# Linear attention over 16 images: keys between queries and outputs on TensorE, the queries' bias in the exponential's shift, the variance by two small matmuls, the query exponentials ahead of the copy

## The reference

```python
def _gn(v, G=32, eps=1e-05): ...          # mean 0, variance 1 in each group of 2 channels
xn = group_norm(x, gn1_w, gn1_b, 32)
qkv = jnp.einsum('oc,bchw->bohw', qkv_w, xn) + qkv_b[None, :, None, None]
q, k, v = jnp.split(qkv, 3, axis=1)       # 8 heads of 16 channels each
q = q.reshape(B, HEADS, DIM_HEAD, n) * scale
q_norm = jax.nn.softmax(q, axis=-1)       # over the 256 pixels
k_norm = jax.nn.softmax(k, axis=-2)       # over the 16 channels of a head
context = jnp.einsum('bhdn,bhen->bhde', k_norm, v)
out = jnp.einsum('bhde,bhdn->bhen', context, q_norm)
out = jnp.einsum('oc,bchw->bohw', out_w, out) + out_b[None, :, None, None]
out = group_norm(out, gn2_w, gn2_b, 1)    # one group: all channels and pixels of an image
return out + res
...
x = x + block(_gn(x), ...)
```

## Time and profile before

| | us |
|---|---|
| median of three runs | 52.71 (52.54 to 52.72) |
| the profiled execution | 52.49 |
| its span, first to last instruction | 50.7 |
| TensorE busy | 42.6 (84%) |
| VectorE busy | 40.6 (80%) |
| ScalarE busy | 33.5 (66%) |
| GpSimd busy | 28.6 (57%) |
| the chain that ended last: TensorE's share | 63% |
| VectorE's share | 25% |

### The profile page before, as it was taken

How to read it: one execution, slowest core, us unless ns; L and a number is a source line. 1 busy time by engine, 2 the same in 40 slices (tenths; PEclk the granted TensorE clock), 3 DMA queues, 4 the chain that set the end, 5 groups by cost and what they waited for, 6 DMA issues and landing times.

```text
span 50.7 us, 1591 instructions
## 1 busy us (share of the span) xinstructions
PE 42.6 (84%) x511; PEld 31.3 (62%) x511; DVE 40.6 (80%) x132; ACT 33.5 (66%) x111; POOL 28.6 (57%) x66
## 2 busy tenths in 40 slices
PE   2999849899989599999999999999999985995000
PEld 2769448656677448866876884886698464834000
DVE  2056999999999995989999999999999698643830
ACT  0183799998586198777958949876494576468300
POOL 5000670088986988899875864884682790222500
PEclk9999999999999999999999999999999999999985
DMA  0598960000000000000110020020020000031122
GB/s 0 138 192 268 347 249 3 0 0 0 0 0 19 0 0 0 0 0 19 65 38 0 11 99 0 13 104 0 0 92 11 0 13 6 0 104 46 57 104 104
DMA packets 2688, 2.66 MB, mean 53 GB/s; under 512 B 244, under 2 KB 2680, under 8 KB 2680
## 3 DMA queue, kind: packets, MB, share of 16 engines
q1 hardware_dynamic: 2528, 2.49, 15.7%
q10 hardware_dynamic: 152, 0.07, 0.6%
HBM read 1.52 MB, written 1.05 MB: 51 GB/s over the span
## 4 chain that ended last, share of the span: by engine, by line
PE 63%; DVE 25%; issue 6%; ACT 1%; POOL 0%; DVEq 0%; ACTq 0%; POOLq 0%
PE o_ps L568 7%; PE o_ps L605 7%; PE q_ps L473 7%; PE o_ps L582 5%; PE v_ps L507 5%; PE q_ps L546 5%; PE k_ps L507 4%; PE q_ps L543 4%; PE v_ps L497 4%; PE k_ps L497 3%; PE o_ps L620 3%; PE o_ps L593 3%; DVE vs L795 3%; DVE res L856 3%; DVE kmx L752 3%
## 5 line engine op out<-in xcount | busy, mean ns | idle before, releaser
L292 POOL TENSOR_TENSOR orstd<-ve,minus_half 128x1 f32<-128x1 f32 x8 | 4.4, 553 | 6.7 <-DVE ve L838 6.7
L273 POOL TENSOR_TENSOR tree<-ek 128x256 f32<-128x256 f32 x7 | 5.1, 725 | 5.4 <-ACT ek L392 5.4
L402 ACT ACTIVATE eq<-q_ps,nqmax 128x256 f32<-128x256 f32 x16 | 7.4, 473 | 0.2 <-DVE nqmax L770 0.2
L415 ACT ACTIVATE fold<-o_ps,rq 128x65 f32<-128x65 f32 x14 | 3.6, 312 | 5.8 <-PE o_ps L582 5.8
L752 DVE TENSOR_REDUCE kmx<-k_ps 128x32 f32<-128x512 f32 x8 | 5.5, 682 | 0.7 <-PE k_ps L507 0.5
L795 DVE TENSOR_TENSOR vs<-v_ps,rks 128x512 f32<-128x512 f32 x8 | 5.5, 691 | 0.3
L507 PE MATMUL k_ps<-w_all,xn 64*128 64x128 f32 x64 | 5.0, 274 | 0.9 <-DVE xn L726 0.9
L473 PE MATMUL q_ps<-ones 128*128 128x512 f32 x12 | 4.7, 550 | 1.0 <-POOL ones L220 1.0
L761 DVE TENSOR_TENSOR ek<-k_ps,kmx 128x512 f32<-128x512 f32 x8 | 5.5, 681 | 0.1
L770 DVE TENSOR_REDUCE nqmax<-q_ps 128x2 f32<-128x512 f32 x8 | 5.4, 678 | 0.0
L426 ACT ACTIVATE osq<-o_ps,nb 128x256 f32<-128x256 f32 x7 | 3.3, 473 | 2.9 <-PE o_ps L605 2.0
(11 more groups left out here) (97 smaller groups left out, 102.0 us busy)
## 6 DMA issues: line engine op xcount, KB each, us to landing
out_dram<-res SPq DMA_DIRECT2D x8, 128.0 KB, 1.7
x_sb<-x_dram SPq DMA_DIRECT2D x1, 512.0 KB, 5.0
x_sb<-x_dram SPq DMA_DIRECT2D x2, 128.0 KB, 2.3
x_sb<-x_dram SPq DMA_DIRECT2D x1, 256.0 KB, 3.9
w_all<-weights_dram SPq DMA_DIRECT2D x1, 224.0 KB, 3.7
mats<-matrices_dram SPq DMA_DIRECT2D x1, 160.0 KB, 4.9
par_avg<-params_dram ACTq DMA_DIRECT2D x1, 67.0 KB, 2.5
brow<-b_qkv_dram ACTq DMA_DIRECT2D x1, 6.0 KB
```

Of the source, the lines that this page charges most:

```text
L273: nc.gpsimd.tensor_tensor(tree[:], e[:, :, 0:8], e[:, :, 8:16], ALU.add).then_inc(tree_step, 1)
L402: last = nc.scalar.activation(eq[:, p % 3, image, :], q_ps[:, image, 0, :], ACT.Exp, bias=nqmax[:, r, image:image + 1], accum_out=qs[:, p ...
```

## The change

Five edits:

1. The queries' bias is no longer added on TensorE: the two matmuls against `scales` go, and that constant with them. The exponential is over pixels, where a constant per channel cancels, so its shift needs only the maximum of the biased queries less the bias. The kernel now makes q_bias once (GpSimd, from a new column of the parameters) and, per pair, `query_shift(p)` on VectorE, (nqmax - q_bias) + q_bias, into qshift, which `query_exp` takes as its bias.
2. query_shift(0) and (1) are called inside `group_variance(2)` and `(3)`, the others behind `minus_mean(i - 2)` in the loop and behind `scale_values` for the last pair.
3. The variance is two matmuls, one per image, with ssq as the stationary side, spread over 64 columns, and one column of the averaging matrix as data. Before, the 128 x 128 matrix was stationary and ssq the data.
4. In TensorE's loop `keys(i + 1)` stands ahead of `means(i - 2)` and `outputs(i - 2)`.
5. In ScalarE's loop `query_exp(i)` stands ahead of `centred(i - 2)`.

```diff
@@ TensorE
                 wait(pe, qexp_ready, p)
-                pe.wait_ge(b_ready, 1)
                 pe.wait_ge(w_ready, 1)
-                pe.wait_ge(scales_ready, 1)
-                for image in range(2):
-                    nc.tensor.matmul(q_ps[:, image, 0, :], bsplit[rows(image), Q], scales[rows(image), 0:PIX],
-                                     start=True, stop=False, skip_group_check=True)
                 for image in range(2):
                     nc.tensor.matmul(q_ps[:, image, 0, :], w_f[rows(image), Q], xn[rows(image), p % 3, :],
-                                     start=False, stop=True, skip_group_check=True).then_inc(q_done[image], 1)
+                                     start=True, stop=True, skip_group_check=True).then_inc(q_done[image], 1)
...
-                nc.tensor.matmul(var_of(p), mats[:, AVG_IMAGE], of(ssq, r),
-                                 start=True, stop=True, skip_group_check=True).then_inc(var_done, 1)
+                for image in range(2):
+                    ins = nc.tensor.matmul(var_of(p)[rows(image), :],
+                                           ssq[rows(image), r:r + 1].broadcast_to([CHANNELS, CHANNELS]),
+                                           mats[rows(image), 2 * P - 1 if image else P:2 * P if image else P + 1],
+                                           start=True, stop=True, skip_group_check=True)
+                ins.then_inc(var_done, 1)
...
                 queries(i)
+                keys(i + 1)
                 means(i - 2)
                 outputs(i - 2)
-                keys(i + 1)
                 context(i - 1)
@@ ScalarE
-                act.wait_ge(qmax_ready, p + 1)
+                act.wait_ge(qshift_ready, p + 1)
...
-                                                bias=nqmax[:, r, image:image + 1],
+                                                bias=qshift[:, r, image:image + 1],
...
                 squares(i - 2)
+                query_exp(i)
                 centred(i - 2)
-                query_exp(i)
@@ VectorE
+            def query_shift(p):
+
+                if not there(p):
+                    return
+                r = p % 2
+                dve.wait_ge(qmax_ready, p + 1)
+                wait(dve, q_bias_ready, 1)
+                wait(dve, qexp_ready, p - 1)
+                nc.vector.tensor_scalar(qshift[:, r, :], nqmax[:, r, :], q_bias[:], q_bias[:], ALU.subtract,
+                                        ALU.add).then_inc(qshift_ready, 1)
@@ GpSimd
-            nc.gpsimd.memset(scales[:].bitcast(F32), QSCALE).then_inc(scales_ready, 1)
...
+            pool.wait_ge(par_in, DMA)
+            nc.gpsimd.tensor_scalar(q_bias[:], par[:, Q_B:Q_B + 1], QSCALE, None,
+                                    ALU.mult).then_inc(q_bias_ready, 1)
```

More of the change, by code:

```diff
@@ L27 @@
 DMA = 16
-GN1_W, GN1_B, OUT_B, GN2_W, GN2_B, LOW_ROW, PARAMS = range(7)
+GN1_W, GN1_B, OUT_B, GN2_W, GN2_B, LOW_ROW, Q_B, PARAMS = range(8)
 TILE = 64
@@ L71, in attention_kernel @@
         ones = sb("ones", [P, 128], F32R)
-        scales = sb("scales", [P, PIX], F32R)
         wjunk = sb("wjunk", [P, CHANNELS])
@@ L102, in attention_kernel @@
         nqmax = sb("nqmax", [HIDDEN, 2, 2])
+        qshift = sb("qshift", [HIDDEN, 2, 2])
+        q_bias = sb("q_bias", [HIDDEN, 1])
         eq = sb("eq", [HIDDEN, 3, 2, PIX])
@@ L132, in attention_kernel @@
         par_in, mats_in, w_in, b_in = (sem(n) for n in ("par_in", "mats_in", "w_in", "b_in"))
-        half_ready, b_zero, ones_ready, scales_ready = sem("half_ready"), sem("b_zero"), sem("ones_ready"), sem("scales_ready")
+        half_ready, b_zero, ones_ready = sem("half_ready"), sem("b_zero"), sem("ones_ready")
         w_ready, bhigh_ready, b_ready = sem("w_ready"), sem("bhigh_ready"), sem("b_ready")
@@ L153, in attention_kernel @@
         ksum_ready, rks_ready, vs_ready = sem("ksum_ready"), sem("rks_ready"), sem("vs_ready")
-        qmax_ready, qexp_ready, rq_ready = sem("qmax_ready"), sem("qexp_ready"), sem("rq_ready")
+        qmax_ready, qshift_ready, q_bias_ready = sem("qmax_ready"), sem("qshift_ready"), sem("q_bias_ready")
+        qexp_ready, rq_ready = sem("qexp_ready"), sem("rq_ready")
         ctx_done, ctxm_ready, fold_done, fold_ready = (
@@ L693, in group_variance @@
                                         ALU.mult).then_inc(mean_x_ready, 1)
+                if g >= 2:
+                    query_shift(g - 2)
                 dve.wait_ge(dev_ready, g + 1)
@@ L768, in query_max @@
                     dve.wait_ge(q_done[image], p + 1)
-                wait(dve, qexp_ready, p - 1)
+                wait(dve, qshift_ready, p - 1)
                 nc.vector.tensor_reduce(nqmax[:, p % 2, :], q_ps[:, :, 0, :], AX.X, ALU.max,
                                         negate=True).then_inc(qmax_ready, 1)
+            def query_shift(p):
[7 more added lines that the diff above has]
+                                        ALU.add).then_inc(qshift_ready, 1)
             def key_norm(p):
@@ L896, in _ @@
                 minus_mean(i - 2)
+                query_shift(i)
                 finish(i - 3)
@@ L911, in _ @@
             scale_values(PAIRS - 1)
+            query_shift(PAIRS - 1)
             output_scale(PAIRS - 4)
@@ L938 @@
     low_row = np.where(c % 64 < 32, 0.0, -1.0).astype(np.float32)
-    params = np.stack([np.concatenate([arr["L0_conv_" + n]] * 2) for n in names] + [low_row], axis=1)
+    params = np.stack([np.concatenate([arr["L0_conv_" + n]] * 2) for n in names] + [low_row, arr["L0_conv_qkv_b"][:HIDDEN]], axis=1)
     group = (c[:, None] // GROUP_CH == c[None, :] // GROUP_CH) / GROUP_CH
```

## The result

The changed kernel took 56.69 us (median of 4 runs, 55.70 to 57.52) beside 52.72 us for the kernel before on the same chip; the ratio is 1.060, with a 95% interval of 1.053 to 1.067. Two of the four runs, 57.30 and 57.52 us at a lower mean clock, are left out of the ratio; the two others, 55.70 and 56.07 us, put the changed kernel near 55.9 us. The profiled execution took 56.07 us with a span of 54.2 us; before it was 52.49 and 50.7. Forecast: 55.7 us (54.4 to 56.6), slower; the median of all four lies 0.09 above that range, the 55.9 within it.

A forecast was written before the change was run, and what follows sets the result against it. TensorE was taken as the bound, 4.27 us a pair. A pair would become 4.78 (2.56 of chain plus 2.22 of need), the end 3.0 later, so 55.5 us profiled and 55.7 us as median; range 54.4 to 56.6.

The forecast's parts named there:

- The pause: TensorE's loop: it stands still 0.85 us in each pair, the variance waiting for ScalarE's copy.
- The need: Loop: from the end of outputs through squares, exponentials and copy to the earliest variance, 2.22 us.
- The cover: TensorE's loop: context and values, the work left between outputs and variance, 1.37 us.
- The pair: Loop: one pair, from variance to variance, takes 4.78 us against 4.27.
- The variance: TensorE: two 64-column matmuls take 0.21 us instead of 0.31; bounds 0.10 and 0.31.
- The start: Ahead of the loop: two shifts on VectorE cost 0.28 us, folds(0) at 17.32 instead of 17.04; bounds 0 and 0.52.
- Behind the loop: After variance(4) at 41.00: vs at 44.50, folds(7) at about 46.9, the end 3.0 us later.
- The bounds: Whole run: pair 4.57 and end 54.5 us at the low side, pair about 4.95 and end 56.6 at the high.
- With 1 and 2 alone: TensorE's pair with only the queries' bias removed and the small variance: 4.27 - 0.32 - 0.10 = 3.85 us.
- A: Rival: TensorE's 0.42 us a pair is really returned, VectorE becomes the bound, 51.5 us; chance 0.07.
- B: Rival: TensorE's rests drop the granted clock to 1.2 GHz in the loop, 57 to 68 us; chance 0.02.
- C: Rival: no measurable change, pause about half (0.43 us), pair 4.3, 52.9 us; chance 0.02.

The follow-up runs named there:

- e9: Changed kernel, but for pairs 0 to 4 the ScalarE copy reads x in SBUF and the variance no longer waits for it: 52.79 us, ratio 1.004.
- e3: Changed kernel with both moves undone (copy ahead of exponentials, keys behind outputs), keeping the shift and the small variance: 52.73 us, ratio 1.003.
- e4: Kernel before with only the query exponentials put ahead of the copy on ScalarE: 54.13 us, ratio 1.027.
- e5: Kernel before with only the keys put ahead of means and outputs on TensorE: 52.91 us, ratio 1.004.
- e7: Kernel before with only the variance done by two small matmuls: 51.57 us, ratio 0.981.
- after2: The changed kernel once more, unedited, beside the others on the same chip: 56.14 us, ratio 1.063.
- v1: e3 with query_shift left out, query_exp taking nqmax of the queries without bias: 51.51 us, ratio 0.978.
- e6: Kernel before with only the queries' bias moved from TensorE into the shift: 53.28 us, ratio 1.012.
- e2: Changed kernel with the keys behind the outputs again on TensorE: four runs of 53.38, 54.48, 55.87 and 56.05 us, not settled.
- e1: Changed kernel with the copy ahead of the query exponentials again on ScalarE: 53.17 us, ratio 1.011.
- e8: Changed kernel with the variance of a pair taken one turn later, behind the keys, and variance_eps and output_scale moved with it: 56.58 us, ratio 1.071.

## Why the prediction was right, point by point

**The pause.** Predicted 0.85 us ahead of each of five variances, released by the copy; it is 1.10 to 1.13, released by the copy, five times. The need was put at 2.22 and is 2.33; 0.09 of the difference is the release, 0.14 where I took 0.05. The cover was put at 1.37 and is 1.23: context ends at 30.24, 0.47 behind the outputs and not 0.61. That e9 without this wait comes to 52.79 us shows that the pause is the cause.

**The pair.** 4.78 predicted, 4.80 measured. From the variance's start to the outputs' end I had 2.56, and it is 2.47 (27.30 to 29.77); so the mechanism was right, but that the sum came within 0.02 is luck: two errors nearly cancel, 0.09 less of TensorE and 0.11 more need.

**The variance.** I took 0.21, from the means' piece of the chain. Folds follow after 0.13 (27.30 to 27.43). The piece of the chain runs from one end to the next; from start to start the means themselves take 0.14 (29.00 to 29.14). The Trainium skill ("TensorEngine Tiling (Array Packing)", Key Properties), whose rule that tiles work in parallel I had set at 0.10, was nearer than my row. Whether the two halves ran at once the runs don't tell, since 0.13 is what the means take too. In the changed kernel's sum the error is worth 0.08 a pair.

**The start.** Folds(0) at 17.32 predicted, 17.79 measured. At 0.47 this is the largest missed size of the sum. The 0.75 over the kernel before has two parts. The second shift moved its successor by 0.34 instead of 0.14; no row says why it costs more than the first. The other 0.42 stand at the end of pow_in, and they are not the first shift's 0.15: pow_in ends with GpSimd's addition, before and after, and the addition came 0.42 later, behind ScalarE's key exponentials (10.01 for 9.57), on an engine whose first squares of the input started at 6.57 for 5.99. e3, with the same instructions up to the loop, had these squares at 6.25, the addition at 10.39, pow_in in 0.40 and folds(0) at 17.49. So the two shifts cost 0.45 there where I had 0.28, inside my bound of 0.52, and some 0.3 came with the later addition, for which the sum had no term. That the change itself delays the input is not shown: the squares start between 5.99 and 6.90 in the four profiles without the shift and its parameter (before, e4, e5, e7), between 6.20 and 6.64 in the others.

**Behind the loop.** Variance(4) at 41.70 for 41.00: 0.47 of it is the start, 0.13 pair 0, 0.10 the four pairs. The new lateness was seen rightly: shift behind vs (45.51), the exponentials until 46.85, variance(5) waiting for them at 46.99, folds(7) at 47.30 for 46.9. From variance(4) to vs it took 3.22 instead of 3.50, so 0.3 of the lateness was made good. The last variance gave nothing back in this profile: 0.38, in a window at 0.53 of the clock; in after2 the same line is 0.28. Ends: 3.6 later for 3.0, 56.07 for 55.5.

**The bounds.** The upper one does not come out of its own terms: 0.10 for the variance and 0.08 make the pair 4.96 before anything is added for the releases, and five such pairs with 0.24 more at the start end near 56.8, not 56.6.

**An argument that failed off the sum.** "With 1 and 2 alone TensorE's pair would be 3.85" is wrong. v1, which has those savings and nothing on VectorE against them, has 4.04, and e6 shows where 0.3 of it stay: in the wait for the fold copy. It did no harm to the forecast, because keys ahead of the means fill this wait (27.43 to 29.00 is 1.57, and the copy needs about 1.0).

**The rivals.** A, faster because the copy doesn't bind, fell. Its point of decision, the copy over within 1.37 of the outputs' end, was the right one: it is over at 2.19. Its next bound was right too: e9 takes the copy's wait away and finds VectorE, 4.22 in A's 3.85 to 4.26, near its upper end. B, the clock: not in the loop's pauses, where the windows say 1.00. But the half clock at the start of the loop in e2's profile is B's mechanism at a place that I had not looked at. C fell with the exponentials' 0.45 each; half the pause would by the sum have been a pair of 4.36 and 53.6 us, not C's 4.3 and 52.9.

## What to carry to other kernels

Before an instruction is moved, write down for the wait behind it how long its releaser needs and how much work covers it; two moves that each fit the slack can overdraw it together, and the loss then comes at once and in every turn. An instruction taken from the engine that is always busy saves only what no other wait takes back: look for the next operand that comes late (here the fold copy, then VectorE) ahead of counting the gain. And ask whether a correction is needed at all: leaving the shift out of e3 gave 1.2 us. Whether another place for it would have been as good was not tried.

## What the runs showed of the hardware

**A small VectorE instruction that meets GpSimd's addition lasts until the addition ends.** The changed kernel, e1 and e3 have the same instructions up to the loop, and in all three pow_in starts at 10.76, while the addition starts when ScalarE's key exponentials are over, which differs from profile to profile. In e3:

```profile
10.76 0.40 DVE L711 TENSOR_SCALAR pow_in<-gvar 128x2 f32<-128x2 f32 x1
```

```profile
10.39 0.75 POOL L274 TENSOR_TENSOR tree<-ek 128x256 f32<-128x256 f32 x1 [3.08 <-ACT ek L396]
```

The addition starts at 10.39 in e3, 10.60 in e1 and 10.70 in the changed kernel; pow_in takes 0.40, 0.60 and 0.69 and ends 0.02 behind the addition each time (11.16, 11.36 and 11.45). In e9 the addition starts at 10.77, pow_in slips in ahead of it in 0.17, and the instruction behind it is the one that takes 0.71. In after2 the addition is early (10.34): there the instruction behind the shift (dev), at 10.38, takes 0.71 where it took 0.15, and without the shift it would have started before the addition. The shift itself takes 0.28 us at 10.20, before the addition starts, 0.57 in e3's loop, and 0.61 in e8, where the rows are:

```profile
34.40 0.61 DVE L787 TENSOR_SCALAR qshift<-nqmax,q_bias 128x2 f32<-128x2 f32 x1
```

```profile
34.27 0.72 POOL L274 TENSOR_TENSOR tree<-ek 128x256 f32<-128x256 f32 x1
```

They end at 35.01 and 34.99. Not every instruction is held: gvar, with one operand in o_ps, takes 0.16 at 10.57 in e3, in the middle of the addition. No run moved the addition by an edit, but the same instruction ends with it wherever it lies. The Trainium skill ("SBUF — State Buffer", "SBUF: two separate sides") has a rule that fits: VectorE and GpSimd share one pair of ports, which GpSimd or a VectorE instruction in a two-port mode or with two inputs in SBUF holds for its whole instruction, whichever starts first, while the other blocks. The rows ahead of the loop agree with it; in e3's loop the shift has the earlier start (32.26 against 32.36) and is held all the same, so who comes first can't always be read from the starts. A small instruction so costs what is left of the large one beside it: 0.29 and 0.33 us more for the shift, some 0.5 for pow_in (0.69 to 0.71 against 0.17).

**The clock at the start of the loop.** e2's profile has the half clock for some 7 us after TensorE, only half busy in the two us before, had rested 0.97; the kernel before rests 0.64 there. The changed kernel rests as long as e2 and kept the full clock in its profile, so the rest alone does not decide, and what does stays open. The pauses of 1.1 us in the loop lowered it in neither profile of the changed kernel.

**From ScalarE's end to TensorE's start** it took 0.14 us in the loop for the copy, against 0.05 from VectorE in the tail before. It is no fixed price of ScalarE: in e6 the means start 0.05 behind the end of the fold copy (31.77 and 31.72). Why the variance takes longer no run shows.
